# Spreading layer 0's projections, attention halves and low parts over its eight score tiles

## The chip, the core and the metric

One core of a Trainium2 chip runs the whole program. The metric is the device time of one execution in microseconds. All times of rows are microseconds from the start of the span unless they say ns. PE is TensorE, PEld its weight loads, DVE VectorE, ACT ScalarE, POOL GpSimd, and SP the engine that issues every DMA (SPq in the rows).

## What is computed

Two layers on x of shape (4, 256, 32, 32), that is 4 images of 256 channels by 1024 positions. All is float32.

```python
# layer 0, per image, xf = x.reshape(256, 1024)
Bm, Cm, Dm = Wb @ xf, Wc @ xf, Wd @ xf
S = softmax(Bm.T @ Cm, axis=-1)          # 1024 x 1024
y = gamma * (Dm @ S.T) + x
# layer 1: group norm, q/k/v projections, 4-head attention over 1024
# positions, output projection, residual; result = y + projection
```

## The kernel before

Every matmul of two float32 operands is split: a high part (the value copied into the type fp32r, made by ACT) and a low part (the value less its high part, made by DVE or POOL). A product is then the three matmuls high·high, low·high and high·low (`products`, L217).

**Layer 0, one image.** The scores are rows of S in eight tiles of 128 rows by 1024 columns (12 matmuls each, `scores0`, L1342), with A = x'(Wb'Wc) made once per image by the four groups a0 to a3 (6 matmuls each, `a_group`). Three tile buffers of PSUM hold them in turn (`score_tile`, L377). A tile then goes a long way round the engines:

1. DVE takes the row maximum (`row_max0`, L894).
2. ACT takes the exponential with its row sum (`exp0`, L677), and DVE the reciprocal (`recip0`, L899).
3. POOL multiplies the tile by it (`normalise0`, L580).
4. DVE transposes it in blocks of 32 by 32 (`turn`, L903, line L911 in rows) into `turned`, of two buffers.
5. SP stores it to DRAM (`store_turned`, L457, issue L460), and after the store has landed loads it back with the blocks in their turned places (`load_turned`, L462, four DMAs at L467) into `pt_lo`.
6. ACT copies it into `pt_hi` (`turn_high_of`, L683, line L685 in rows). The low part is the difference (`turn_difference`, L395, line L397 in rows): POOL makes it for tiles 0, 1, 2, 4, 5 and 6 of an image (`POOL_LOWS`), DVE for tiles 3 and 7 (`DVE_LOW`, L915).

Four tiles make one half of the result's columns. The groups av0 and av1 (24 matmuls each, `values`, L1350) use tiles 0 to 3, av2 and av3 tiles 4 to 7. Before av0, PE waits for the low parts of four tiles, before av2 for those of eight. DVE takes each group's result out of PSUM, adds the residual and takes statistics (`result`, L1057, lines L1063 and L1068), and SP stores it (`store_result`, L474).

All groups other than scores share two PSUM banks in turn (`place_groups`, L128), so that a group waits until the one before the last has been taken out (`bank_free`, L1245).

**The order** is written out by hand for each engine. PE runs a score tile and behind it one entry of `SCORES0` (L57): av2 and av3 of the image before, in halves, behind tiles 0 to 3, the projections d0 to d3 (12 matmuls each, D = Wd x, `project_d`) behind tiles 4 to 7. Then comes `TAIL0` (L62): av0 in quarters, av1, and the next image's a0 to a3, for which PE waits until the next image's x is split (`x_part_high`, L712, on ACT, and `x_part_low`, L1007, on DVE). The last image has `TAIL0_LAST` (L63) instead: av0, av1, then the first projections of layer 1 (qk0 to qk5) with av2 in thirds and av3 between them, then the first two score tiles of layer 1 (s0, s1). Each qk group is restacked by SP into `q_st` or `k_st` by four DMAs (`restack`, L438, issue L451), and the buffer of qk holds two groups, so that ACT waits before the third for the first's DMAs (`chunk_high`, L740).

ACT's order in layer 0 is `image0` at L755: exponentials, behind those of steps 2 to 5 the high parts of tiles 0 to 3, the d high parts behind steps 4 to 7, and after step 7 the high part of tile 4, x, tiles 5 and 6, then a0, tile 7, a1 to a3. POOL's is `image0` at L624: normalise tile t, and behind t = 3, 4, 5 the low parts of tiles 0, 1, 2, and 4, 5, 6 at the end. DVE's is `image0` at L1052: at step s the reciprocal of tile s-1, then up to step 4 the turning of tile s-1 before the maximum of tile s, from step 5 on the maximum before the turning. SP's is `image0` at L478: up to tile 3 each tile is stored and loaded, from tile 4 on the load of tile t-1 is issued behind the store of tile t. The first image has its own order, because nothing of an image before it exists.

Layer 1 (`image1`) runs 32 score tiles per image and is not touched.

## Time and profile before

| what | value |
|---|---|
| median of 3 runs | 727.3 us (724.44 to 727.85) |
| profiled execution, its own time | 727.05 us |
| its span | 725.3 us |
| PE busy | 681.8 us (94%) |
| PE weight loads busy | 567.3 us (78%) |
| DVE busy | 552.1 us (76%) |
| ACT busy | 454.9 us (63%) |
| POOL busy | 288.5 us (40%) |
| chain that ended last, by engine | PE 65%, DMA 11%, DVE 10%, issue 5%, ACT 4%, SPq 4% |

A busy share is an average over the whole span. Layer 0 takes about the first 278 us, layer 1 the rest. To see what bounds layer 0, its four images have to be looked at one by one. An engine's idle time is written in brackets behind the instruction that ended it, with what released it. The span is 1.75 us shorter than the execution's own time, and the difference lies around it.

### The profile page before, as it was taken

How to read it: one execution, taken by the hardware profiler on the slowest of the kernel's cores; microseconds unless marked ns; L12 is line 12 of the kernel's file. 1: busy time of each engine (PE TensorE's matmuls, PEld its weight loads, DVE VectorE, ACT ScalarE, POOL GpSimd, SP SyncE). 2: the span in 40 equal slices, each digit the busy share in tenths (PEclk: the TensorE clock that was granted, in tenths of full speed). 3: DMA queues.
4: the chain of work that ended last, by engine and by line, in shares of the span. 5: the costliest groups of instructions: out<-in, count | busy, mean ns of one | idle time of the engine just before them, and what ended most of it. 6: DMA issues, size and time to landing. Idle time of an engine off the chain costs nothing.

```text
span 725.3 us, 11325 instructions
## 1 busy us (share of the span) xinstructions
PE 681.8 (94%) x3632; PEld 567.3 (78%) x3632; DVE 552.1 (76%) x854; ACT 454.9 (63%) x788; POOL 288.5 (40%) x238
## 2 busy tenths in 40 slices
PE   4948999899999978999999999999999999999996
PEld 3746788688788766887888987887888888888885
DVE  3548556656765735999888889888889988889994
ACT  4344334325524324798777778877779877778883
POOL 0144234415516511356524356433346523334531
PEclk9989999899999999999999999999999999999999
DMA  8256557635845866700165401165501145501011
GB/s 272 89 156 197 171 189 224 194 127 192 240 166 175 243 158 150 203 1 1 44 160 132 131 16 45 44 139 129 154 14 43 29 119 129 130 15 44 7 47 36
DMA packets 52143, 86.32 MB, mean 119 GB/s; under 512 B 6016, under 2 KB 24704, under 8 KB 52096
## 3 DMA queue, kind: packets, MB, share of 16 engines
q1 hardware_dynamic: 52096, 85.75, 41.5%
q8 instruction: 22, 0.36, 0.2%
q14 instruction: 25, 0.20, 0.1%
HBM read 35.40 MB, written 25.17 MB: 83 GB/s over the span
## 4 chain that ended last, share of the span: by engine, by line
PE 65%; DMA 11%; DVE 10%; issue 5%; ACT 4%; SPq 4%; POOL 0%; ACTq 0%; DVEq 0%; POOLq 0%
PE acc L1241 33%; PE scores L1241 17%; PE trans L1275 14%; DMA turn_scratch<-turned 4%; DMA pt_lo<-turn_scratch 4%; SPq L467 3%; DVE negmax L887 2%; DVE turned L911 2%; DMA w_later<-in_wlater 1%; DVE negmax L896 1%; DVE pt_lo L930 1%; PE trans L1241 1%; ACT prob L694 1%; ACT pt_hi L704 1%; DMA k_st<-qk 1%
## 5 line engine op out<-in xcount | busy, mean ns | idle before, releaser
L593 POOL TENSOR_SCALAR prob<-prob,rsum 128x1024 f32<-128x1024 f32 x127 | 143.3, 1128 | 264.3 <-DVE rsum L892 264.3
L704 ACT ACTIVATE pt_hi<-trans 128x512 fp32r<-128x512 f32 x256 | 140.2, 595 | 62.9 <-PE trans L1275 60.2
L930 DVE TENSOR_TENSOR pt_lo<-trans,pt_hi 128x512 fp32r<-128x512 f32 x256 | 163.7, 680 | 3.1 <-ACT pt_hi L704 2.8
L887 DVE TENSOR_REDUCE negmax<-scores 128x1 f32<-128x1024 f32 x128 | 155.1, 1212 | 8.3 <-PE scores L1241 6.8
L694 ACT ACTIVATE prob<-scores,negmax 128x1024 f32<-128x1024 f32 x128 | 143.3, 1120 | 13.4 <-DVE negmax L887 11.8
L1275 PEld LDWEIGHTS trans<-ident,prob 128*128 128x128 f32 x1024 | 117.2, 140 | 28.7 <-DVE pt_lo L930 5.3
L1275 PE MATMUL trans<-ident,prob 128*128 128x128 f32 x1024 | 135.7, 274 | 4.1 <-DVE pt_lo L930 3.4
L1241 PE MATMUL scores<-k_st,q_st 128*128 128x512 f32 x512 | 137.8, 391 | 0.9 <-issue 0.5
L1241 PEld LDWEIGHTS scores<-k_st,q_st 128*128 128x128 f32 x512 | 95.8, 188 | 22.3 <-ACT prob L694 1.0
L1241 PE MATMUL acc<-pt_hi,v_st 128*128 128x512 f32 (+1 forms) x264 | 106.7, 407 | 1.9 <-DVE pt_lo L930 1.9
L1241 PE MATMUL acc<-pt_lo,v_st 128*128 128x512 f32 (+1 forms) x264 | 101.0, 385 | 0.0
L397 POOL TENSOR_TENSOR pt_lo<-pt_lo,pt_hi 128x1024 fp32r<-128x1024 f32 x24 | 59.9, 2498 | 18.2 <-ACT pt_hi L685 18.2
L1241 PE MATMUL acc<-pt_hi,d_hi 128*128 128x512 f32 x128 | 52.5, 410 | 7.6 <-DVE qk L1048 3.9
L685 ACT ACTIVATE pt_hi<-pt_lo 128x1024 fp32r<-128x1024 f32 x32 | 33.8, 1056 | 39.9 <-DMA pt_lo<-turn_scratch 39.7
L1241 PEld LDWEIGHTS acc<-pt_hi,v_st 128*128 128x128 f32 x264 | 49.8, 189 | 9.1 <-DVE pt_lo L930 2.1
L1241 PEld LDWEIGHTS acc<-pt_lo,v_st 128*128 128x128 f32 x264 | 50.0, 189 | 7.1
L583 POOL TENSOR_SCALAR prob<-prob,rsum 128x1024 f32<-128x1024 f32 x16 | 18.0, 1127 | 84.9 <-DVE rsum L901 84.9
L1241 PE MATMUL acc<-pt_lo,d_hi 128*128 128x512 f32 x128 | 51.6, 403 | 0.0
L1241 PE MATMUL acc<-pt_hi,d_lo 128*128 128x512 f32 x128 | 51.5, 403 | 0.0
L1241 PE MATMUL scores<-x_hi,a_hi 128*128 128x512 f32 x96 | 37.9, 395 | 1.0 <-ACT prob_more L680 1.0
L583 POOL TENSOR_SCALAR prob_more<-prob_more,rsum 128x1024 f32<-128x1024 f32 x16 | 18.0, 1126 | 52.1 <-DVE rsum L901 52.1
L680 ACT ACTIVATE prob<-scores,negmax 128x1024 f32<-128x1024 f32 x12 | 13.4, 1116 | 40.2 <-DVE negmax L896 40.2
(143 smaller groups left out, 1168.6 us busy)
## 6 DMA issues: line engine op xcount, KB each, us to landing
turn_scratch<-turned SPq DMA_DIRECT2D x32, 512.0 KB, 3.3
pt_lo<-turn_scratch SPq DMA_DIRECT2D x128, 128.0 KB, 3.4
k_st<-qk SPq DMA_DIRECT2D x64, 256.0 KB, 4.6
q_st<-qk SPq DMA_DIRECT2D x64, 128.0 KB, 2.4
x_raw<-in_x SPq DMA_DIRECT2D x8, 512.0 KB, 5.7
y_out<-in_x SPq DMA_DIRECT2D x16, 256.0 KB, 3.6
y_scratch<-y_out SPq DMA_DIRECT2D x16, 256.0 KB, 2.9
y_in<-y_scratch SPq DMA_DIRECT2D x4, 1024.0 KB, 7.5
```

What stands on the lines that cost most here:

```text
L397: return engine.tensor_tensor(turned_tile(pt_lo, t), turned_tile(pt_lo, t).bitcast(F32), turned_tile(pt_hi, t).bitcast(F32), ALU.subtract)
L467: sp.dma_start(dst.rearrange("c (q n) -> c q n", q=QUADS), blocks[g]).then_inc(turn_moved[t % 4], 16)
L583: nc.gpsimd.tensor_scalar(p, p, rsum[:, t % 4:t % 4 + 1], 1.0, ALU.mult, ALU.mult)\
L593: nc.gpsimd.tensor_scalar(p, p, rsum[:, t % 2:t % 2 + 1], 1.0, ALU.mult, ALU.mult)\
L685: nc.scalar.activation(turned_tile(pt_hi, t), turned_tile(pt_lo, t).bitcast(F32), ACT.Copy)\
L694: nc.scalar.activation(prob[:, t % 2, :], scores[:, t % 2, :], ACT.Exp, bias=negmax[:, t % 2:t % 2 + 1], scale=1.0, accum_out=rowsum[:, t ...
L704: nc.scalar.activation(pt_block(pt_hi, (t // 4) % 2, t, h), trans[:, h, :].rearrange("p (j n) -> p j n", n=P), ACT.Copy).then_inc(pt_high, 1)
L887: nc.vector.tensor_reduce(negmax[:, t % 2:t % 2 + 1], scores[:, t % 2, :], AX_X, ALU.max, negate=True).then_inc(max_ready, 1)
L911: nc.vector.transpose(turned[:, t % 2, :], prob_tile(t).rearrange("p (j g c) -> p g j c", g=QUADS, c=QUAD))\
L930: nc.vector.tensor_tensor(pt_block(pt_lo, slot, t, h), trans[:, h, :].rearrange("p (j n) -> p j n", n=P), pt_block(pt_hi, slot, t, h).bitc ...
L1241: ins = nc.tensor.matmul(dst, w, m, start=(starts and n == 0), stop=(stops and n == len(pairs) - 1))
L1275: ins = nc.tensor.transpose(trans[:, h, b * P:(b + 1) * P], prob[:, t % 2, j * P:(j + 1) * P], ident[:, :])
```

## The change

- PE: behind tile 4 come d0 and d1, behind tile 5 d2 and d3, behind tiles 6 and 7 the two halves of this image's own av0. The tail begins with av1. In the last image qk0 to qk3 follow av1 without a part of av2 between them, then av2, qk4, av3, qk5. The group a0 waits for the first half of the next x alone, a2 for the second.
- SP: in every image but the first, each tile is stored and then loaded before the next one is stored. In the first image load t-1 stands behind store t up to tile 3, from then on as in the others. The other DMAs take other places in the queue, and av0's result is stored right behind tile 7's load.
- Low parts: all eight on POOL, tile s-2 behind the normalising of tile s, except tile 3 (`URGENT`), which stands ahead of the normalising of tile 5. DVE makes none.
- ACT: the high part of tile s-2 behind the exponential (and the d parts) of step s, except tile 3, which stands ahead of the exponential of step 5. Tile 4 stands behind the exponential of step 6, tile 5 behind that of step 7, tile 6 behind the next x, tile 7 behind a1 (qk1).
- DVE: at step s the reciprocal of tile s-1, the d low parts (two at step 5, two at step 6), the turning of tile s-1, then the maximum of tile s. In the first image up to step 4 the maximum comes before the turning. av0's result is taken out right behind the next x (last image: behind the four parts of h).

```diff
-SCORES0 = [("prev_av2", 0, 2), ("prev_av2", 1, 2), ("prev_av3", 0, 2), ("prev_av3", 1, 2), "d0", "d1", "d2", "d3"]
-D_STEPS = [4, 5, 6, 7]
+BEHIND_SCORES0 = {0: [("prev_av2", 0, 2)], 1: [("prev_av2", 1, 2)], 2: [("prev_av3", 0, 2)], 3: [("prev_av3", 1, 2)],
+                  4: ["d0", "d1"], 5: ["d2", "d3"], 6: [("av0", 0, 2)], 7: [("av0", 1, 2)]}
+D_STEPS = {4: (0, 1), 5: (2, 3)}
-TAIL0 = FIRST_HALF + ["av1", "next_a0", "next_a1", "next_a2", "next_a3"]
-TAIL0_LAST = FIRST_HALF + ["av1", "next_qk0", "next_qk1", ("av2", 0, 3), "next_qk2", ("av2", 1, 3), "next_qk3",
-                           ("av2", 2, 3), "av3", "next_qk4", "next_qk5", "s0", "s1"]
+TAIL0 = ["av1", "next_a0", "next_a1", "next_a2", "next_a3"]
+TAIL0_LAST = ["av1", "next_qk0", "next_qk1", "next_qk2", "next_qk3", "av2", "next_qk4", "av3", "next_qk5", "s0", "s1"]
-POOL_LOWS, DVE_LOW = (0, 1, 2), 3
+URGENT = 3
...
@@ SP, image0
-                    if t == 4 and not first:
-                        store_result(i - 1, 3)
-                        sp.wait_ge(y_stored, FREE_CREDIT + i * 64)
-                        load_result_residual(i, 1)
                     store_turned(i, t)
-                    if t < 4 and not first:
-                        load_turned(i, t)
-                    elif t % 4 > 0:
+                    if first and t in (1, 2, 3):
                         load_turned(i, t - 1)
-                    if t == 7 or (first and t == 3):
+                    if not first or t >= 3:
                         load_turned(i, t)
                     if t == 1 and not first:
                         store_result(i - 1, 2)
+                    if t == 3 and not first:
+                        store_result(i - 1, 3)
+                    if t == 5 and not first:
+                        sp.wait_ge(y_stored, FREE_CREDIT + i * 64)
+                        load_result_residual(i, 1)
+                store_result(i, 0)
@@ POOL, image0
+                    behind = t - HIGH_BEHIND
+                    if behind == URGENT:
+                        turn_low_of(t0, behind)
                     normalise0(t0, t)
-                    if t - 3 in POOL_LOWS:
-                        turn_low_of(t0, t - 3)
+                    if behind >= 0 and behind != URGENT:
+                        turn_low_of(t0, behind)
...
-                for t in POOL_LOWS:
-                    turn_low_of(t0, t + 4)
+                for t in range(T0_IMAGE - HIGH_BEHIND, T0_IMAGE):
+                    turn_low_of(t0, t)
@@ ACT, image0
+                    behind = s - HIGH_BEHIND
+                    if behind == URGENT:
+                        turn_high_of(i, behind)
                     exp0(t0, s)
-                    if HIGH_BEHIND <= s < HIGH_BEHIND + 4:
-                        turn_high_of(i, s - HIGH_BEHIND)
+                    for n in D_STEPS.get(s, ()):
+                        high(d_part(d_hi, n), plan, f"d{n}")
+                    if behind >= 0 and behind != URGENT:
+                        turn_high_of(i, behind)
...
-                turn_high_of(i, 4)
                 if not last:
                     for half in range(X_HALVES):
                         x_part_high(i + 1, half)
-                turn_high_of(i, 5)
                 turn_high_of(i, 6)
-                if last:
-                    turn_high_of(i, 7)
...
-                    if name == "next_a0":
+                    if name in ("next_a1", "next_qk1"):
                         turn_high_of(i, 7)
@@ DVE, image0
-                    if 1 <= s <= 4:
+                    for n in D_STEPS.get(s - 1, ()):
+                        low(d_part(d_lo, n), d_part(d_hi, n), plan, f"d{n}", highs + plan.until(f"d{n}", KINDS0))
+                    dense = first and s <= 4
+                    if s >= 1 and not dense:
                         turn(i, s - 1)
...
                     row_max0(t0, s)
-                    if s == HIGH_BEHIND + 4:
-                        turn_low_of(t0, DVE_LOW)
-                    if s > 4:
+                    if s >= 1 and dense:
                         turn(i, s - 1)
...
+                result("av0", i)
@@ PE, image0
-                        pe.wait_ge(turn_low_pool, 6 * of + 3 * (half + 1))
-                        pe.wait_ge(turn_low, 2 * of + half + 1)
+                        pe.wait_ge(turn_low, T0_IMAGE * of + 4 * (half + 1))
                     if name == "av0":
-                        evacuated(plan.number(f"d{part}"))
+                        evacuated(plan.number(f"d{2 * part + 1}"))
...
-                        if n == 0:
-                            pe.wait_ge(x_split, X_HALVES * (i + 2))
+                        if n % 2 == 0:
+                            pe.wait_ge(x_split, X_HALVES * (i + 1) + n // 2 + 1)
```

## Rows read from the trace of the kernel before

**Rows 1.** Windows by image: stretch, length, busy us by engine, PEclk, DMA share, GB/s.

```profile
18.48:79.59 61.11, 47.91 (x218) 38.62 (x216) 36.35 (x45) 24.84 (x36) 23.52 (x14) 0.94 0.53 155
79.59:142.44 62.85, 59.21 (x265) 48.21 (x264) 39.19 (x45) 23.98 (x34) 24.11 (x14) 0.95 0.59 188
142.44:200.23 57.79, 57.07 (x265) 46.07 (x264) 37.02 (x45) 23.80 (x34) 24.25 (x14) 1.00 0.62 194
200.23:278.61 78.38, 72.54 (x329) 58.80 (x328) 42.36 (x69) 25.80 (x39) 27.68 (x19) 0.98 0.66 189
```

**Rows 2.** Timeline of PE, chosen matmuls: start us, us, what, [idle before <-releaser].

```profile
12.05 0.47 PE L1241 MATMUL acc<-x_hi,wbc_hi 128*128 128x512 f32 x1 [2.50 <-DVE wbc_lo L1029]
...
50.88 0.58 PE L1241 MATMUL acc<-wd_hi,x_hi 128*128 128x256 f32 x1 [8.13 <-DVE d_lo L1016]
...
85.15 0.39 PE L1241 MATMUL scores<-x_hi,a_hi 128*128 128x512 f32 x1
...
87.90 0.40 PE L1241 MATMUL acc<-pt_hi,d_hi 128*128 128x512 f32 x1
...
90.74 0.39 PE L1241 MATMUL trans<-x_hi,a_hi 128*128 128x512 f32 x1
...
104.66 0.28 PE L1241 MATMUL acc<-wd_hi,x_hi 128*128 128x256 f32 x1
...
106.09 0.40 PE L1241 MATMUL trans<-x_hi,a_hi 128*128 128x512 f32 x1
...
134.05 0.79 PE L1241 MATMUL acc<-x_hi,wbc_hi 128*128 128x512 f32 x1 [3.20 <-DVE y_out L1063]
...
259.57 0.76 PE L1241 MATMUL acc<-pt_hi,d_hi 128*128 128x512 f32 x1 [3.92 <-DVE qk L1048]
```

**Rows 3.** Timeline of ACT: high parts behind a load; a chunk of layer 1.

```profile
37.53 1.06 ACT L685 ACTIVATE pt_hi<-pt_lo 128x1024 fp32r<-128x1024 f32 x1 [3.27 <-DMA pt_lo<-turn_scratch]
...
112.85 1.06 ACT L685 ACTIVATE pt_hi<-pt_lo 128x1024 fp32r<-128x1024 f32 x1 [0.83 <-DMA pt_lo<-turn_scratch]
...
125.41 1.06 ACT L685 ACTIVATE pt_hi<-pt_lo 128x1024 fp32r<-128x1024 f32 x1 [3.37 <-DMA pt_lo<-turn_scratch]
...
264.61 0.69 ACT L746 ACTIVATE qk<-acc,vec 128x512 fp32r<-128x512 f32 x1 [5.95 <-PE acc L1241]
```

**Rows 4.** Timeline of SP: store and load of a tile, a later load, restacks.

```profile
104.93 0.34 SPq L460 DMA_DIRECT2D turn_scratch<-turned  x1
...
108.39 1.73 SPq L467 DMA_DIRECT2D pt_lo<-turn_scratch  x4
...
119.15 2.07 SPq L467 DMA_DIRECT2D pt_lo<-turn_scratch  x4
...
259.45 5.23 SPq L451 DMA_DIRECT2D q_st<-qk  x8
```

**Rows 5.** Timeline of DVE: turnings of images 0 and 1, x_lo, h_lo.

```profile
25.51 1.25 DVE L911 STREAM_TRANSPOSE turned<-prob 128x1024 f32<-128x1024 f32 x1 [1.45 <-POOL prob L583]
...
30.67 1.25 DVE L911 STREAM_TRANSPOSE turned<-prob 128x1024 f32<-128x1024 f32 x1 [1.36 <-POOL prob L583]
...
103.67 1.23 DVE L911 STREAM_TRANSPOSE turned<-prob_more 128x1024 f32<-128x1024 f32 x1
...
123.10 1.25 DVE L911 STREAM_TRANSPOSE turned<-prob_more 128x1024 f32<-128x1024 f32 x1 [0.34 <-POOL prob_more L583]
...
127.45 5.89 DVE L1010 TENSOR_TENSOR x_lo<-x_raw,x_hi 128x1024 fp32r<-128x1024 f32 x2 [3.10 <-ACT x_hi L715]
...
246.34 2.46 DVE L370 TENSOR_TENSOR h_lo<-y_in,h_hi 128x512 fp32r<-128x512 f32 x4
```

**Rows 6.** By line: x_lo low parts at the start; pt_lo on DVE, on POOL.

```profile
L1010 DVE TENSOR_TENSOR x_lo<-x_raw,x_hi x2: 1215/1220/1226, 10.1 to 11.9; 128x1024 fp32r<-128x1024 f32 x2
...
L397 DVE TENSOR_TENSOR pt_lo<-pt_lo,pt_hi x8: 1214/1217/1762, 56.4 to 257.5; 128x1024 fp32r<-128x1024 f32 x8
...
L397 POOL TENSOR_TENSOR pt_lo<-pt_lo,pt_hi x24: 2340/2406/3338, 41.2 to 255.1; 128x1024 fp32r<-128x1024 f32 x24
```

More of the change, by code:

```diff
@@ L327, in build @@
         turn_low = sem("turn_low")
-        turn_low_pool = sem("turn_low_pool")
         transposed = sem("transposed")
@@ L1383, in image0 @@
                         norm_group(plan, "gn1", 0, gn_sqdev, 1)
[L1384 to L1387 removed]
+                    for g in BEHIND_SCORES0[s]:
+                        if g in D_GROUPS:
+                            project_d(D_GROUPS.index(g))
+                        elif g[0] == "av0":
+                            values(g[0], i, *g[1:])
+                        elif not first:
+                            values(g[0], i - 1, *g[1:])
                 for g in TAIL0_LAST if last else TAIL0:
```

29 lines of the change are left out of this document (5 added, 24 removed).

## The prediction, made before the changed kernel was run

> **What bounds the kernel now.** The page says PE 94% busy, so I looked for PE's idle time. The windows by image [rows 1] show it in layer 0: from an image's first score tile to the next one's it takes 61.11, 62.85 and 57.79 us, and 78.38 us for the last image up to layer 1's first scores. The third has PE busy for 57.07 us at full clock, so 57 us is near what an image costs when nothing waits.
>
> The PE timeline [rows 2] gives the pieces. A score tile takes 2.75 us (85.15 to 87.90), half an av group 2.84, a d group 1.43 (104.66 to 106.09), so an a group of half as many matmuls as a score tile takes 1.4. Per image: 8 x 2.75 + 4 x 5.68 + 4 x 1.43 + 4 x 1.4 = 56.0. What is above it are stalls: 8.13 us before d2 in image 0, 3.20 before a0 in image 1, 3.92 in the last image, where the DVE, queued behind tile 7's low part, is late with qk. [...]
>
> The ACT and SP rows tell why. Tile 3's high part starts at 112.85, that is 33.3 us into its image [rows 3]: store at 104.93, landed and load issued at 108.39, load in at 112.85, 4.5 us later [rows 4]. Tile 4's load, sharing the DMA engines with another store, needs 6.3 us (119.15 to 125.41) [rows 3, 4]. x's high and low parts stand behind it. That is the stall before a0.
>
> **The change, part by part.** I write times from the image's first score tile.
>
> *PE's order.* No matmul is added. Tiles 4 to 7 now come every 5.6 us (2.75 + 2 x 1.43, or 2.75 + 2.84) instead of 4.2. S5 ends at 30.7, S6 at 36.3.
>
> *Tile 3 ahead.* Tiles 0 to 3 keep their pace, order and queue, so tile 3's load is in at 33.1 as before. ACT could start exponential 5 at 32.1 (S5's end and a maximum of 1.2), but takes tile 3 first: 33.1 to 34.1, the exponential to 35.4. POOL takes low 3 first too, 2.40 us [rows 6]: 34.2 to 36.6. Normalising 5 follows to 37.7, turning 5 from 37.9 to 39.1. On DVE it would have ended at 36.3, so tile 5 is 2.8 us late. PE can start av0 at 36.8, a stall of only 0.5.
>
> *The round.* From tile 5 on the maximum stands behind the turning of the tile before, so a tile costs a whole round: maximum, exponential, reciprocal, normalising, turning. The rounds of image 0, in that order already, take 5.16 us (25.51 to 30.67) [rows 5]. PE gives 5.6, so only 0.4 is regained per tile. Turning 7 ends at 39.1 + 2 x 5.2 = 49.5. Before, it ended at 44.8 (124.35 less 79.59) [rows 5].
>
> *x and av0's result.* The x parts come behind turning 7. Low 5 sits on POOL from 48.4 (behind normalising 7) to 50.8. An x_lo takes 1.22 alone; the two of image 1 took 5.89 beside POOL's lows [rows 5, 6], so they wait for each other. I take: the first ends 1.1 behind low 5, at 51.9, the second at 53.1 (bounds 52.0 with no such wait, 55.4 with the 5.89). Then av0's result, 0.75: 53.9, and a0 may start at 54.0. PE, with av0 from 36.8, S7 and av1, is done at 50.9. **A stall of 3.1 us before a0**, nearest to the row of 3.20, so I price it like that one: next image at 54.0 + 8.4 = 62.4. Images 1 and 2 come to 124.8, before 120.6: +4.2.
>
> *Image 0.* With the maximum ahead of the turning, exponentials 1 and 2 come 2.5 and 5 us earlier, and then ACT stands in front of tile 0's high part. Its load goes out at about 30 instead of 32.3, so ACT has it at 35 to 36 instead of 37.53 [rows 3]. Exponential 4 is at 38.5, d0's low part at 41.3, and d2 starts at about 42.4 instead of 50.88: the stall of 8.13 becomes one of about 4. Tile 3's load goes out at 44, in at 49; low 3 ends near 52.5, a second stall of about 4 before av0. Then rounds of 5.2: turning 7 ends at 65.3, a0 starts near 70.5, image 1 near 76.5 instead of 79.6: -3.1. This counts 1.4 to 1.7 of slow matmuls behind each of the two.
>
> *Last image.* The four low parts of h (2.46 alone, 246.34) [rows 5] now stand between turning 7 (48.9, gn0 and gn1 included) and av0's result. No row shows them beside a POOL low that started first: bounds 0 and 2.4, I take 1.5 as for x_lo. qk0 starts at 54.3. [...] qk0 to qk3 run together, 5.6 us, and then av2 needs qk2's bank. qk2's high part waits for qk0's DMAs: 5.2 us from issue to ACT (259.45 to 264.61) [rows 3, 4]. av2 starts about 11 us behind qk0, a stall of 3.6 where 3.92 was, with the same clock loss. From there 2 x 5.68 + 2 x 1.4 = 14.2. Sum 80.5 against 78.4 (200.2 to 278.6): +2.1.
>
> *At nothing:* DVE rid of two lows (1.22 each [rows 6]) wins nothing, since it waits for tiles. The a2 gate, the moved result stores and residual loads (an issue of 0.4 to 0.9 each) lie beside the round on a queue that needs 3.5 + 1.75 per tile of 5.6; without that slack each would delay a tile by itself. Layer 1 starts from the same state.
>
> Sum: -3.1 + 4.2 + 2.1 = +3.2 on 727.05, the profiled execution, which lies 0.25 under the median of the three runs. **Forecast 730.2.**
>
> **The rivals.**
>
> *The clock holds.* The stall of 3.1 lies between the idle times that kept the clock (2.50) and lost it (3.20) [rows 2]. If it keeps it, images 1 and 2 take 60.1 (54.0 + 5.6 + 0.5) and the last image loses 0.7 less: 730.2 - 4.6 - 0.7 = 725. [...]
>
> *No stall at all.* Tile 3's data come early enough that ACT loses nothing, and the rounds of tiles 6 and 7 fit. Then images 1 and 2 take 56.6 (-7.4), image 0 58 (-3.1), the last image about 76 (-2.4): 714. Against it: tile 3's way is in the old trace at 33.3, and nothing of the change shortens it. Half of that would give 721.
>
> *Loads as slow as tile 4's.* Tile 3's load takes 6.3 instead of 4.5 because results, residuals and the next x share the engines with it. It decides from any microsecond on: ACT, POOL and PE all stand behind this one load, so its 1.8 us come four times, in image 0 also for tile 0: 730.2 + 4 x 1.8 + 1.3 = 739. For it: 6.3 in the row. Against it: tile 3 itself, at 4.5, had the same neighbours.
>
> **How the numbers follow.** Forecast 40%, clock holds 25%, no or half a stall 17%, slow loads 18%. About 0.5%, 3.6 us, is what a measurement of this kernel can tell from no change: faster is below 723.7, slower above 730.9. The forecast's own range is 727 to 733 (bounds of x_lo and h_lo), a third of it slower, so slower is 0.18 + 0.14 = 0.32. Faster is 0.17 and a little of the clock case: 0.20. Same 0.48. The range goes from 719 to 738: it leaves out the full case without stalls and the end of the slow one.
>
> **What would show it.** Right: in images 1 and 2 ACT waits for a DMA before tile 3's high part and exponential 5 behind it; the turnings of tiles 5, 6 and 7 are 5.2 apart and the last ends 49 to 50 into the image; PE is idle for about 3 us before a0, released by DVE's y_out; image 0 has two stalls of about 4 us instead of one of 8; in the last image av2's first matmul waits for DVE qk. Wrong: no idle time before a0, or tile 3's high part starting clearly before 33; then I have its load or the order behind it wrong, and the time goes toward 714.

## The result, and the profile after

| what | before | after |
|---|---|---|
| median of 5 runs | 726.87 us (724.44 to 727.85) | 731.24 us (729.96 to 732.35) |
| ratio, 95% interval | | 1.0064 [1.0041, 1.0087] |
| profiled execution, its span | 727.05, 725.3 us | 732.35, 730.6 us |

The changed kernel is 0.64% slower, just over the 0.5% that the prediction took as what can be told. Two more runs of before put its median at 726.87 instead of 727.3. The forecast was 730.2 with a range of 719 to 738. Five executions taken for the experiments were disturbed (one 1.8% above the fastest of its kernel, the others 17% to 138%), and the medians below leave them out.

The page of the changed kernel, its busy line, its chain and ACT's high parts of loaded tiles:

```profile
PE 684.2 (94%) x3632; PEld 568.4 (78%) x3632; DVE 541.3 (74%) x846; ACT 453.3 (62%) x788; POOL 304.2 (42%) x246
...
PE 63%; DVE 9%; DMA 8%; issue 7%; POOL 5%; ACT 5%; SPq 2%; ACTq 0%; DVEq 0%; POOLq 0%
...
L686 ACT ACTIVATE pt_hi<-pt_lo 128x1024 fp32r<-128x1024 f32 x32 | 33.8, 1055 | 56.2 <-DMA pt_lo<-turn_scratch 56.2
```

POOL is busier by 15.7 us and DVE less by 10.8; the eight low parts that moved are worth 19.2 and 9.7 us by [rows 6]. In the chain, POOL with 5% is new (0% before), and the DMA share fell from 11% to 8%. ACT spends 56.2 us standing before tiles' loads. Where the time lies is seen again in the windows by image, the columns being those of [rows 1]:

```profile
20.15:77.10 56.95, 48.13 (x217) 39.32 (x216) 32.71 (x41) 23.52 (x35) 25.48 (x15) 0.94 0.52 157
77.10:139.42 62.32, 58.62 (x266) 47.21 (x265) 35.06 (x42) 23.15 (x34) 28.05 (x16) 0.97 0.57 182
139.42:200.75 61.33, 57.15 (x266) 45.96 (x264) 34.56 (x42) 23.38 (x34) 27.98 (x16) 1.00 0.58 189
200.75:283.93 83.18, 73.92 (x329) 59.28 (x328) 41.23 (x67) 26.97 (x40) 34.34 (x22) 0.96 0.64 190
```

Against [rows 1] the images changed by -4.16, -0.53, +3.54 and +4.80 us. The first score tile starts at 20.15 instead of 18.48, +1.67. What follows image 3 takes 446.67 instead of 446.69. That makes the +5.3 of the span. The third window is the plainest: PE is busy for 57.15 us at a granted clock of 1.00, as before (57.07), but the image takes 61.33 us.

The timeline of PE of the changed kernel, the matmuls before which it stood idle:

```profile
43.95 0.58 PE L1230 MATMUL acc<-wd_hi,x_hi 128*128 128x256 f32 x1 [4.41 <-DVE d_lo L1011]
54.34 0.79 PE L1230 MATMUL acc<-pt_hi,d_hi 128*128 128x512 f32 x1 [3.18 <-POOL pt_lo L395]
...
114.56 0.50 PE L1230 MATMUL acc<-pt_hi,d_hi 128*128 128x512 f32 x1 [0.28 <-POOL pt_lo L395]
131.79 0.51 PE L1230 MATMUL acc<-x_hi,wbc_hi 128*128 128x512 f32 x1 [2.85 <-DVE y_out L1058]
143.51 0.50 PE L1230 MATMUL acc<-pt_hi,d_hi 128*128 128x512 f32 x1 [1.21 <-POOL pt_lo L395]
...
194.50 0.50 PE L1230 MATMUL acc<-x_hi,wbc_hi 128*128 128x512 f32 x1 [2.36 <-DVE y_out L1058]
...
240.04 0.50 PE L1230 MATMUL acc<-pt_hi,d_hi 128*128 128x512 f32 x1 [1.30 <-POOL pt_lo L395]
256.90 0.47 PE L1230 MATMUL acc<-h_hi,wq_hi 128*128 128x512 f32 x1 [2.50 <-DVE y_out L1058]
267.65 0.77 PE L1230 MATMUL acc<-pt_hi,d_hi 128*128 128x512 f32 x1 [4.47 <-DVE qk L1043]
```

The 8.13 us before d2 in image 0 [rows 2], with another 1.72 before av0 (at 60.09 in the kernel before), became 4.41 and 3.18. Images 1 and 2 both have a stall before a0 now, and one of 1.21 stands before the av2 that runs in image 2, where there was none. The last image has three; before, it had 3.92 before av2 and 1.43 before av0 (at 241.31).

The rows behind the stall before a0 in image 1, of ACT, POOL and DVE:

```profile
110.89 1.06 ACT L686 ACTIVATE pt_hi<-pt_lo 128x1024 fp32r<-128x1024 f32 x1 [3.39 <-DMA pt_lo<-turn_scratch]
111.86 1.10 ACT L681 ACTIVATE prob<-trans,negmax 128x1024 f32<-128x1024 f32 x1
```

```profile
112.03 2.40 POOL L395 TENSOR_TENSOR pt_lo<-pt_lo,pt_hi 128x1024 fp32r<-128x1024 f32 x1 [2.04 <-ACT pt_hi L686]
114.42 1.11 POOL L581 TENSOR_SCALAR prob<-prob,rsum 128x1024 f32<-128x1024 f32 x1
...
126.44 2.41 POOL L395 TENSOR_TENSOR pt_lo<-pt_lo,pt_hi 128x1024 fp32r<-128x1024 f32 x1 [0.43 <-ACT pt_hi L686]
```

```profile
115.57 1.25 DVE L910 STREAM_TRANSPOSE turned<-prob 128x1024 f32<-128x1024 f32 x1 [0.71 <-POOL prob L581]
...
120.89 1.25 DVE L910 STREAM_TRANSPOSE turned<-prob_more 128x1024 f32<-128x1024 f32 x1 [1.53 <-POOL prob_more L581]
...
126.05 1.25 DVE L910 STREAM_TRANSPOSE turned<-prob_more 128x1024 f32<-128x1024 f32 x1 [1.37 <-POOL prob_more L581]
127.35 3.72 DVE L1005 TENSOR_TENSOR x_lo<-x_raw,x_hi 128x1024 fp32r<-128x1024 f32 x2
```

ACT stands before tile 3's load with exponential 5 behind it, POOL makes low 3 before it normalises 5, and so the turning of 5 starts 38.5 us into the image (115.57 less 77.10). The rounds that follow are 5.32 and 5.16 apart. This is the chain that the prediction drew. Beside it SP shows what it did not draw, the tail of the tiles on its queue:

```profile
122.88 0.90 SPq L469 DMA_DIRECT2D y_out<-in_x  x2
123.89 0.36 SPq L458 DMA_DIRECT2D turn_scratch<-turned  x1
129.69 1.75 SPq L465 DMA_DIRECT2D pt_lo<-turn_scratch  x4
131.56 0.36 SPq L458 DMA_DIRECT2D turn_scratch<-turned  x1
```

Tile 6 was turned at 122.14. Its store went out at 123.89, behind the residual load, and had landed only at 129.69, 5.8 us later; tile 7, turned at 127.30, was stored at 131.56. Over layer 0 the waits of SP for a store to land went from the first of these lines, of before, to the second, of after (us in all, times, longest):

```profile
SPq L467 <- DMA turn_scratch<-turned: 43.6, 21, 3.5
```

```profile
SPq L465 <- DMA turn_scratch<-turned: 90.4, 29, 5.3
```

### The profile page after: what moved, and what is told of

It reads as the page before. It is cut to its first block, busy times and chain, and to the rows that moved or that the text cites. A ratio compares the mean times of both kernels' runs of the same rounds, so it can differ in the third digit from the quotient of the medians.

```text
span 730.6 us, 11320 instructions
## 1 busy us (share of the span) xinstructions
PE 684.2 (94%) x3632; PEld 568.4 (78%) x3632; DVE 541.3 (74%) x846; ACT 453.3 (62%) x788; POOL 304.2 (42%) x246
## 4 chain that ended last, share of the span: by engine, by line
PE 63%; DVE 9%; DMA 8%; issue 7%; POOL 5%; ACT 5%; SPq 2%; ACTq 0%; DVEq 0%; POOLq 0%
PE acc L1230 32%; PE scores L1230 15%; PE trans L1264 14%; DMA turn_scratch<-turned 5%; POOL pt_lo L395 3%; DMA pt_lo<-turn_scratch 2%; DVE turned L910 2%; DVE negmax L886 2%; SPq L465 2%; DVE pt_lo L925 1%; PE trans L1230 1%; DVE negmax L895 1%; ACT prob L695 1%; DMA x_raw<-in_x 1%; POOL prob_more L581 1%
## 5 line engine op out<-in xcount | busy, mean ns | idle before, releaser
L695 ACT ACTIVATE prob<-scores,negmax 128x1024 f32<-128x1024 f32 x128 | 143.3, 1119 | 13.4 <-DVE negmax L886 11.8
L395 POOL TENSOR_TENSOR pt_lo<-pt_lo,pt_hi 128x1024 fp32r<-128x1024 f32 x32 | 76.5, 2389 | 52.2 <-ACT pt_hi L686 52.1
L686 ACT ACTIVATE pt_hi<-pt_lo 128x1024 fp32r<-128x1024 f32 x32 | 33.8, 1055 | 56.2 <-DMA pt_lo<-turn_scratch 56.2
L1230 PE MATMUL acc<-pt_hi,d_hi 128*128 128x512 f32 x128 | 53.6, 419 | 11.3 <-POOL pt_lo L395 6.8
L1230 PEld LDWEIGHTS acc<-pt_lo,v_st 128*128 128x128 f32 x264 | 49.9, 189 | 7.1
L900 DVE RECIPROCAL rsum<-rowsum 128x1 f32<-128x1 f32 x32 | 5.2, 162 | 50.7 <-ACT prob L681 28.4
L1230 PEld LDWEIGHTS acc<-pt_hi,d_hi 128*128 128x128 f32 x128 | 24.9, 195 | 20.1 <-POOL pt_lo L395 5.3
L581 POOL TENSOR_SCALAR prob<-prob,rsum 128x1024 f32<-128x1024 f32 x16 | 18.0, 1123 | 53.6 <-DVE rsum L900 53.6
L1230 PE MATMUL scores<-x_hi,a_lo 128*128 128x512 f32 x96 | 37.5, 391 | 0.0
```

Of the source, the lines that this page charges most:

```text
L395: return engine.tensor_tensor(turned_tile(pt_lo, t), turned_tile(pt_lo, t).bitcast(F32), turned_tile(pt_hi, t).bitcast(F32), ALU.subtract)
L581: nc.gpsimd.tensor_scalar(p, p, rsum[:, t % 4:t % 4 + 1], 1.0, ALU.mult, ALU.mult)\
L686: nc.scalar.activation(turned_tile(pt_hi, t), turned_tile(pt_lo, t).bitcast(F32), ACT.Copy)\
L695: nc.scalar.activation(prob[:, t % 2, :], scores[:, t % 2, :], ACT.Exp, bias=negmax[:, t % 2:t % 2 + 1], scale=1.0, accum_out=rowsum[:, t ...
L1230: ins = nc.tensor.matmul(dst, w, m, start=(starts and n == 0), stop=(stops and n == len(pairs) - 1))
```

## The experiments

Two limits had to be told apart. **The round**: DVE comes late to x and to av0's result because turning 7 is late (maximum behind the turning, tile 3 ahead of 5, POOL's low parts). **The queue**: with one tile at a time, tiles 6 and 7 are late, and what ACT and PE have behind them waits. **The cover** is a third reading: PE has 8.5 us of work between tile 7's scores and a0 (half of av0, and av1) where it had 11.4. The experiments ran in three groups, each on one chip with the kernel before beside it: e1, e2, e4 and e5, then e6, e3, e7 and e8, then e10, e9, e11 and e12. The kernel before had medians of 726.07, 725.12 and 725.8 in them. Image lengths are from each profile, from one image's first score tile to the next one's.

| kernel | images 0 to 3, us | median | ratio to before |
|---|---|---|---|
| after | 56.95, 62.32, 61.33, 83.18 | 731.24 | 1.0064 [1.0041, 1.0087] |
| e1 av0's result early | 57.37, 63.44, 59.68, 83.62 | 731.61 | 1.0078 [1.0049, 1.0107] |
| e2 tile 3 not ahead | 62.78, 59.16, 59.88, 80.35 | 732.21 | 1.0091 [1.0067, 1.0115] |
| e4 residual load late | 57.16, 62.27, 59.32, 82.21 | 731.31 | 1.0060 [1.0031, 1.0088] |
| e3 old last tail | 57.33, 62.87, 61.47, 83.50 | 732.72 | 1.0115 [1.0056, 1.0175] |
| e7 maximum first | 57.62, 62.81, 60.95, 83.43 | 732.98 | 1.0109 [1.0059, 1.0160] |
| e8 DVE's lows back | 57.10, 62.04, 60.30, 81.60 | 729.75 | 1.0070 [1.0040, 1.0099] |
| e10 av0 behind tile 7 | 58.66, 61.50, 61.46, 80.06 | 731.93 | 1.0105 [1.0064, 1.0147] |
| e9 three places | 55.41, 64.47, 60.70, 83.21 | 731.93 | 1.0090 [1.0056, 1.0124] |
| before + e5 | 59.23, 58.88, 57.79, 78.06 | 723.20 | 0.9960 [0.9929, 0.9991] |
| before + e11 | 65.67, 67.49, 65.95, 86.24 | 752.30 | 1.0372 [1.0337, 1.0408] |
| before + e12 | 56.42, 58.30, 57.30, 74.80 | 714.93 | 0.9854 [0.9828, 0.9880] |

**e1: take av0's result before tile 7's last steps on DVE**

```diff
@@ DVE, image0, behind the maximum of tile s
+                    if s == T0_IMAGE - 1:
+                        result("av0", i)
...
-                result("av0", i)
```

> The changed kernel with one edit: the DVE takes av0's result behind the maximum of tile 7, while it would wait for the exponential, instead of behind both x_lo parts. My theory (the DVE's order at the image's end makes the stall before a0): the first x_lo part ends about 1.1 us before the second, and 0.75 of the result goes too, so the stalls of 2.85 and 2.35 us before a0 in images 1 and 2 fall to about 1.1 and 0.8, image 1 no longer loses the clock (another 1.9), and the last image's stall before qk0 falls by 0.75: in all 5 us less than the changed kernel, about 726 us. Rival (the slow loads of tiles 6 and 7 are the real limit and hold the next image's av2): the stall before a0 goes, but comes back in front of av2, and the time stays within 1.5 us of 731.

The stall before a0 fell from 2.85 and 2.36 us to 1.06 and 0.94, released by x_lo. A new one of 2.85 and 1.44 came later in the a groups. In image 1, PE and ACT:

```profile
137.49 0.80 PE L1231 MATMUL acc<-x_hi,wbc_hi 128*128 128x512 f32 x1 [2.85 <-DVE a_lo L1011]
```

```profile
135.16 1.06 ACT L686 ACTIVATE pt_hi<-pt_lo 128x1024 fp32r<-128x1024 f32 x1 [5.72 <-DMA pt_lo<-turn_scratch]
```

ACT stood before tile 6's load for 5.72 us, with a's high parts behind it, and until a0's high and low parts are made a2 has no PSUM bank. So a0 started 53.0 us into the image instead of 54.7, but a2 at 59.3 instead of 59.4: the queue lies close behind the first limit, and the edit is worth nothing in the median.

**e2: tile 3 has no place ahead**

```diff
-URGENT = 3
+URGENT = None
```

> The changed kernel with tile 3's high and low parts behind step 5's exponential and normalising, like the other tiles. My theory (ACT standing in front of tile 3's load before exponential 5 delays the rounds of tiles 5 to 7 by about 2.5 us): turning 7 ends 2 to 3 us earlier in its image, the stall before a0 shrinks to about 1.2 us, but av0 waits 1.3 us more for low 3, so the time changes by less than 2 us against 731. Rival (the urgent place pays for itself, because av0 stands on low 3): av0's stalls grow by more than the stall before a0 shrinks, 734 us or more.

Images 1 and 2 are 3.16 and 1.45 us shorter: the stall before a0 is 0.81 and 0.80, at the price of 1.42 before av0. This shows that tile 3's place carries most of that stall. The last image is 2.8 us shorter too. Image 0 pays most of it back, 5.8 us more (4.37 before av0, then 3.07 before a0), and the median does not tell this kernel from the changed one.

**e4: the residual load behind the image's last tile**

```diff
@@ SP, image0
-                    if t == 5 and not first:
-                        sp.wait_ge(y_stored, FREE_CREDIT + i * 64)
-                        load_result_residual(i, 1)
+                if not first:
+                    sp.wait_ge(y_stored, FREE_CREDIT + i * 64)
+                    load_result_residual(i, 1)
```

> The changed kernel with the second residual load (512 KB) issued behind tile 7's load instead of in front of tile 6's store. My theory: tile 6's store, 5.8 us from issue to landing in image 1, falls to about 3.5 and tile 7's load lands 2 us earlier, which takes away the stalls of 0.4, 1.2 us before av2 and part of the 4.5 us before av2 of the last image (1 us, because there qk2's bank comes free only 0.3 us before low 7): about 728.5 us. Rival (the slow landing has another cause, the loads of tile 5 or the order of DRAM reads and writes): no change, 731.

SP's rows of image 1, in place of those shown of after:

```profile
123.44 0.36 SPq L458 DMA_DIRECT2D turn_scratch<-turned  x1
127.02 1.73 SPq L465 DMA_DIRECT2D pt_lo<-turn_scratch  x4
```

The store of tile 6 lands in 3.58 us, not 5.8. ACT has tile 6 at 131.43 instead of 134.21, and the stall before av2 in image 2 is gone (-2.0 us for that image, 1.2 of them this stall). The stall before a0 is there as before, 2.47 and 2.37. So the residual load is what made tile 6 late, and it has no part in a0's stall. In the median nothing is left of it that the intervals could show.

**e5: in the kernel before, image 0's maximum ahead of the turning**

```diff
@@ DVE, image0
-                    if 1 <= s <= 4:
+                    dense = first and s <= 4
+                    if 1 <= s <= 4 and not dense:
                         turn(i, s - 1)
...
-                    if s > 4:
+                    if s > 4 or (s >= 1 and dense):
                         turn(i, s - 1)
```

> The kernel before with one part of the change alone: in image 0, up to tile 4, the maximum ahead of the turning. My theory (half of image 0's gain of 4 us comes from this order, until ACT stands in front of tile 0's load): exponential 3 comes 1.5 us earlier, tile 4's 3 to 5 us, the stall of 8.13 us before d2 falls to 4 to 5 us and the image ends about 3 us earlier: 724 us. Rival (the gain of image 0 comes from the places of d0 to d3 and of the SP queue): less than 1 us, 726.5.

Image 0 is 1.9 us shorter, but not by the way that was expected: the stall before d2 is 7.92 us where it was 8.13. The gain lies before two score tiles (0.62 and 0.98 became one of 0.36) and before av0 (1.72 became 0.61). The median is 2.9 us under that of before, and the interval ends just below 1. The 58.88 of image 1 against 62.85 can hardly be the edit's, which touches image 0 alone: its stall before a0 was 0.50 in this execution, 3.20 in that of before. The two profiled executions lie 6.2 us apart where the medians lie 2.9 apart, so a part of that difference is chance, and the 62.85 is a doubtful base for image 1. Of the 4.16 us that image 0 gained in the changed kernel this order gives about half; e12 shows where the rest is.

**e6: e1 and e4 together**

```diff
@@ SP, image0: as e4
@@ DVE, image0: as e1
```

> The two edits of e1 and e4 together on the changed kernel: av0's result behind the maximum of tile 7, and the second residual load behind tile 7's load. Alone, neither moved the time. My theory now (two queues end the image almost at once: the DVE with av0's result, and ACT, which stands in front of tile 6's load before it can take a0 out; each hides the other): images 1 and 2 need both, and take about 59 us each instead of 62.3 and 61.3, the last image about 82, in all 725 to 727 us. Rival (each edit has a cost of its own that ate its gain, such as av0's result in front of tile 7's reciprocal): 731 or more again.

Median 728.4 us, ratio 1.0045 [1.0013, 1.0078], the lowest of the variants of the changed kernel but not told apart from its 1.0064, and above the 725 to 727 us that two limits hiding each other should have given. Its profiled execution took 738.0 us, so its images are not read, and it has no row in the table.

**e3: the old tail in the last image**

```diff
-TAIL0_LAST = ["av1", "next_qk0", "next_qk1", "next_qk2", "next_qk3", "av2", "next_qk4", "av3", "next_qk5", "s0", "s1"]
+TAIL0_LAST = ["av1", "next_qk0", "next_qk1", ("av2", 0, 3), "next_qk2", ("av2", 1, 3), "next_qk3",
+              ("av2", 2, 3), "av3", "next_qk4", "next_qk5", "s0", "s1"]
```

> The changed kernel with the last image's tail in the old order, av2 in thirds between the qk groups. My theory (av2 stands on tile 7's low part, ready at 266.5 in the changed kernel, 0.3 us before qk2's bank): av2 starts about 1 us earlier, but qk2 and qk3, 2.8 us of PE, now lie behind the stall and not in it, so the last image takes 1 to 3 us more, 732 to 734 us. Rival (the bank and the restacks are the limit of the new order): the stall before av2 falls from 4.5 to 3 us or less and the kernel is 2 us faster, 729.

The last image takes 83.50, +0.3. A part of av2 now waits 5.84 us for POOL's low 7 where the whole of it waited 4.47 for qk. av2 starts 2.4 us earlier, 64.5 us into the image, but qk2 and qk3, 2.8 us of PE's work, now lie behind the stall and not ahead of it. The order of the tail is not what costs.

**e7: maximum ahead of the turning for tiles 5 to 7 too**

```diff
-                    dense = first and s <= 4
+                    dense = (first and s <= 4) or s > 4
```

> The changed kernel with the maximum ahead of the turning from step 5 on, as in the kernel before. The forecast's theory (the round of 5.2 us per tile makes the end of the image late): turning 7 ends about 3 us earlier and the stall before a0 goes, 726 us. Rival, which a walk over the durations gives: tile 5's load lands when it did, ACT stands in front of it before the next x's high parts, and the x_lo parts and the stall before a0 stay as they are, 730 to 732 us, with turning 7 about 3 us earlier all the same.

Turning 7 starts 48.4 us into image 1 (48.95 in the changed kernel), and the stall before a0 is 2.42 and 1.95. Only 0.5 us came back, because tile 7's scores stand behind half of av0 on PE: DVE waited 3.02 us for them before maximum 7. The order of maximum and turning makes the rounds 5.2 us long, but PE's own spacing of 5.6 is next to it, and so the order alone costs 0.5. Nor did a0 gain by it (55.3 us into image 1, 54.7 in the changed kernel), for x then waited for ACT, which had stood 1.97 us before tile 5's load with x's high parts behind it:

```profile
128.21 3.71 DVE L1005 TENSOR_TENSOR x_lo<-x_raw,x_hi 128x1024 fp32r<-128x1024 f32 x2 [1.21 <-ACT x_hi L716]
```

This is the rival that stood beside the expectation.

**e8: low parts 3 and 7 back on DVE**

```diff
@@ POOL, image0
-                for t in range(T0_IMAGE - HIGH_BEHIND, T0_IMAGE):
+                for t in (6,):
...
@@ DVE, image0
                     row_max0(t0, s)
+                    if s == 5:
+                        turn_low_of(t0, 3)
...
+                    if name in ("next_a1", "next_qk1"):
+                        turn_low_of(t0, 7)
```

> The changed kernel with the low parts of tiles 3 and 7 on the DVE again (1.2 us instead of 2.4): tile 3's behind the maximum of tile 5, tile 7's behind a1 (qk1). The forecast's theory (low 3 on POOL holds normalising 5 by about 1 us and so every later round): turning 7 ends 1 us earlier in images 1 and 2, the stall before av0 goes (0.3 to 1.3 us) and the one before a0 falls by 1 us; tile 7's low part is ready 1.2 us earlier: 727 to 729 us. Rival (POOL has room, where the low parts are made does not matter): 731.

The stall before av0 in image 0 is 2.02 (3.18), that before av2 in the last image 3.61 (4.47). The stall before a0 stays, 3.34 and 1.83. The images together take 261.04 us against 263.78, but the ratio overlaps that of the changed kernel: what POOL's 2.4 us for a low part against DVE's 1.2 costs is at most near 3 us, and not resolved.

**e10: both halves of av0 behind tile 7**

```diff
-                  4: ["d0", "d1"], 5: ["d2", "d3"], 6: [("av0", 0, 2)], 7: [("av0", 1, 2)]}
+                  4: ["d0", "d1"], 5: ["d2", "d3"], 6: [], 7: [("av0", 0, 2), ("av0", 1, 2)]}
```

> The changed kernel with both halves of av0 behind tile 7, so that score tile 7 follows tile 6 at once. New theory (cover): what counts is how much PE work lies behind score tile 7, because its maximum, exponential, normalising and turning, the next x and av0's result come after it one by one; the spreading cut that cover from 11.4 us (av0 and av1) to 8.5. Alone this edit gives the cover back, but the round of 5.2 us per tile, with the maximum behind the turning, keeps turning 7 where it is (49 to 50 us into the image): images 1 and 2 stay at 61 to 62.5 us, the time at 730 to 732. Rival (the maximum order never mattered, PE's place of tile 7 alone set turning 7): turning 7 moves 2 us or more ahead and the kernel gets to 727 or less.

The cover is 11.4 us again. The stalls before av0 are gone (0.70 us is left in image 0), and those before a0 are 5.09, 3.45 and 2.88. a0 of image 1 starts 54.0 us into it, 54.7 in the changed kernel. More cover only moves PE's idle time, since a0 waits for DVE, and turning 7 still starts at 48.75 into the image. By itself, cover is not the reason; e9 needs it together with e7's order and an earlier x.

**e9: e10, e7, and tile 5's high part behind x on ACT**

```diff
@@ PE: as e10; DVE: as e7; ACT, image0
-                    if behind >= 0 and behind != URGENT:
+                    if behind >= 0 and behind != URGENT and behind != 5:
...
+                turn_high_of(i, 5)
                 turn_high_of(i, 6)
```

> The changed kernel with three places put back: both halves of av0 behind tile 7, the maximum ahead of the turning from step 5 on, and the next x's high parts ahead of tile 5's. Cover theory: turning 7 starts 44 to 45.5 us into images 1 and 2 instead of 49, x is split by 48, and there is no stall before a0. The loads of tiles 6 and 7, one by one on the queue at 5.3 us or more a tile, then come to the front: a stall of 1 to 3 us before the next image's av2. Images 1 and 2 take 58 to 60 us, the time is 725 to 728. Rival (something else holds a0: the low parts on POOL, or tile 6's load through ACT): a stall of 2 us or more stays before a0, 730 or more.

Here the round gives way, as DVE of image 1 (from 74.85) shows:

```profile
121.27 1.25 DVE L911 STREAM_TRANSPOSE turned<-prob_more 128x1024 f32<-128x1024 f32 x1 [2.33 <-POOL prob_more L581]
122.44 2.31 DVE L1006 TENSOR_TENSOR x_lo<-x_raw,x_hi 128x1024 fp32r<-128x1024 f32 x2
```

Turning 7 starts at 46.4, the x parts are done at 49.9, and there is no stall before a0. But ACT and PE:

```profile
132.44 1.06 ACT L686 ACTIVATE pt_hi<-pt_lo 128x1024 fp32r<-128x1024 f32 x1 [7.58 <-DMA pt_lo<-turn_scratch]
```

```profile
134.76 0.79 PE L1231 MATMUL acc<-x_hi,wbc_hi 128*128 128x512 f32 x1 [5.31 <-DVE a_lo L1012]
```

All that was won stands in one wait, 7.58 us of ACT for tile 6. The store of tile 6 was issued at 121.92, right behind the residual load, and had landed at 127.97. The stall has only moved from a0 to a2, and its release from the round to the queue.

**e11: in the kernel before, the change's queue order alone**

```diff
@@ SP, image0
-                    if t < 4 and not first:
-                        load_turned(i, t)
-                    elif t % 4 > 0:
+                    if first and t in (1, 2, 3):
                         load_turned(i, t - 1)
-                    if t == 7 or (first and t == 3):
+                    if not first or t >= 3:
                         load_turned(i, t)
```

> The kernel before with the change's order of stores and loads alone (each tile stored and then loaded, the other DMAs where they were). Theory: with score tiles every 4.2 us a queue that needs 5.3 us a tile falls behind; tile 4's load comes about 1 us earlier and shortens the stall before a0, tile 7's comes 2 to 4 us later and holds a0 to a3 through ACT and the next av2: 0 to 5 us slower, 729 us. Rival (this order is what gives the change its gain in image 0): 2 us or more faster, 723 or less.

It costs 26.5 us (752.3 less 725.8), where 0 to 5 had been expected. PE of the old order gives a tile every 4.2 us, and the loads of tiles 4 to 7 go out at 123.87, 130.35, 135.81 and 141.21, that is 5.4 to 6.5 apart. The waits of SP, the same line as the two above, and the worst stall of PE:

```profile
SPq L467 <- DMA turn_scratch<-turned: 89.9, 29, 5.1
```

```profile
284.05 0.76 PE L1239 MATMUL acc<-pt_hi,d_hi 128*128 128x512 f32 x1 [10.23 <-DVE qk L1046]
```

The same 90 us of waits are in the changed kernel, where tiles come every 5.6 us and layer 0 is 21.6 us shorter than here. So one tile at a time costs 26.5 us in PE's old order, and spreading the tiles, with what goes with it, nearly pays for it. What it costs in the spread order was not measured.

**e12: the kernel before, with image 0's order, the d parts first and the last image's tile 7 behind qk1**

```diff
@@ DVE, image0: as e5
@@ ACT, image0
                     exp0(t0, s)
+                    if s in D_STEPS:
+                        n = D_STEPS.index(s)
+                        high(d_part(d_hi, n), plan, f"d{n}")
                     if HIGH_BEHIND <= s < HIGH_BEHIND + 4:
                         turn_high_of(i, s - HIGH_BEHIND)
...
-                    if s in D_STEPS:
-                        n = D_STEPS.index(s)
-                        high(d_part(d_hi, n), plan, f"d{n}")
...
-                if last:
-                    turn_high_of(i, 7)
...
-                    if name == "next_a0":
+                    if name in ("next_a0", "next_qk1"):
                         turn_high_of(i, 7)
@@ DVE, image0: low 7 behind qk1 instead of ahead of qk0
```

> The kernel before with the parts of the change that the runs speak for: the maximum ahead of the turning in image 0 up to tile 4, and ACT's d high parts ahead of the high part of a tile; in the last image the high and low part of tile 7 behind qk1's instead of ahead of qk0's. Theory: in image 0 d0 and d1 are taken out before ACT stands in front of tile 2's load, the stall of 7.9 us before d2 falls to 3 or 4, and the first restacks of layer 1 go out 3 us earlier: 3 to 5 us less than the run with the maximum's place alone (723), 718 to 720 us. Rival (the stall only moves on to av0, which stands on tile 3's low part): 722 to 723 us.

It beats both kernels, and its own forecast of 718 to 720: 714.93 us (712.88 to 716.13), 10.9 under before. Its windows, columns as in [rows 1], and the largest stall left outside image 0:

```profile
17.57:73.99 56.42, 47.28 (x218) 38.22 (x216) 37.57 (x45) 24.84 (x36) 23.27 (x14) 0.97 0.58 166
73.99:132.29 58.30, 56.88 (x265) 46.01 (x264) 38.11 (x45) 23.81 (x34) 23.88 (x14) 1.00 0.62 198
132.29:189.59 57.30, 56.67 (x266) 46.03 (x264) 38.15 (x45) 23.84 (x34) 24.37 (x14) 1.00 0.66 202
189.59:264.39 74.80, 71.12 (x329) 57.71 (x328) 43.91 (x69) 25.82 (x39) 28.83 (x19) 1.00 0.69 199
```

```profile
246.74 0.47 PE L1238 MATMUL acc<-pt_hi,d_hi 128*128 128x512 f32 x1 [3.09 <-DVE pt_lo L397]
```

Three parts of it are the change's own: image 0's order, the d parts ahead of a tile's high part, tile 7 behind qk1. Without the new queue order they gain 1.5%. Image 0 differs from that of e5 by the d parts alone, and takes 56.42 instead of 59.23. PE is idle there for 9.1 us instead of 10.5, with 1.72 before d2, 2.84 before d3 and 3.92 before av0 in place of 7.92 before d2; the other half is PE's busy time, 47.28 instead of 48.75 us, at a granted clock of 0.97 instead of 0.91. Image 1, at 58.30, had 0.51 us before a0, much as in e5, so its 4.6 us against the kernel before are not put down to these edits. In the last image, where tile 7's place counts too, it is 74.80 against 78.06; how these 3.3 us divide was not tried.

## Why the prediction was right, and where it was not

Times are again from an image's first score tile.

**The sum: close, and in part by luck.** In the profiled execution image 0 came out 1.1 us under its term and images 1 and 2 together 1.2 under, the last image was 2.7 over, and 1.7 at the start stood in no term. These nearly cancel; the medians differ by +4.4 where +3.2 was forecast.

**Tile 3 and the round: right.** Tile 3 reached ACT at 33.8 (forecast 33.1), PE started av0 at 37.5 (36.8), the rounds took 5.32 and 5.16 (5.2), turning 7 ended at 50.2 (49.5), and a0 started at 54.7 (54.0). The 0.7 of tile 3 went through unchanged. e2 shows the cause: with tile 3 not ahead the stall before a0 is 0.8. In image 2 tile 3 came at 34.7 and a0 at 55.1. x's low parts took 3.72 us beside POOL's low 5 (forecast 3.6 from turning 7's end to theirs), and 2.31 in e9, where none ran beside them. The 5.89 of the kernel before, which the forecast kept as a bound, had a second low part of POOL that began inside the pair:

```profile
129.46 2.80 POOL L397 TENSOR_TENSOR pt_lo<-pt_lo,pt_hi 128x1024 fp32r<-128x1024 f32 x1 [0.50 <-ACT pt_hi L685]
```

**The stall before a0: right in size, its clock in one image of two.** Forecast 3.1 us; measured 2.85 and 2.36. Priced like the row of 3.20, the next image should have come 8.4 us behind a0: in the kernel before it did (134.05 to 142.44, the a matmuls 0.43 us apart and the granted clock 0.50 until 139.7), where the forecast counts 5.6 for four a groups that wait for nothing. It came 7.63 behind in image 1 (granted clock 0.78 over them) and 6.25 in image 2 (1.00). That is the rival in which the clock holds, in one image. The two took 123.65 against 124.8. Image 1's 62.32 against 62.4 hides two misses, a0 0.7 us later and the way behind it 0.8 shorter.

The chance of that rival was set with a row that was misread. The 2.50 us at 12.05 [rows 2] do not show a pace that was kept, for it was low before them. The matmuls ahead of that wait, such as the last one, come 0.21 us apart for 256 columns, where a d group of the same size takes 1.43 for twelve, 0.12 apart (the granted clock reads 1.00 in both stretches):

```profile
9.14 0.41 PE L1241 MATMUL acc<-wc_lo,wb_hi 128*128 128x256 f32 x1
```

Behind it they come 0.23 us apart for 512 columns. So their pace per column about doubled by the end of that wait, and no row of the kernel before bounds from below what a stall may last.

**Image 0: right in its times, short in its cause.** d2 started 23.8 us behind the first score tile (forecast 23.9), av0 34.2 (34.0), turning 7 ended at 46.8 (46.8), a0 started at 50.9 (52.0). The image took 56.95 against 58.0; the 1.1 lies between turning 7's end and a0, where x_lo and av0's result took 4.1 us and the sum had 5.2. But the prediction names only the maximum ahead of the turning. e5 has that alone and keeps 7.92 us before d2; the d parts ahead of a tile's high part on ACT, which the change also has, are what takes them away (e12).

**The last image: the sum of terms failed by 2.7 us.** Forecast 80.5, measured 83.18. The step that failed is "turning 7 (48.9, gn0 and gn1 included)": it ended at 51.9. The forecast's own 49.5 for images 1 and 2 had no gn0 in it, so the 48.9 was too early from the start, and in the kernel before the parts of h began 46.1 us into the last image, where turning 7 ended 44.8 into image 1. Against the 50.2 of image 1 the last image is 1.7 later, and tile 3 brought that: its high part came at 35.7 instead of 33.8. PE's idle time for gn0 is 0.72 of the 1.9; the store took 4.14 us to land instead of 3.34, which is 0.8, and the load 0.4 more. The rounds behind it stayed at 5.15 us each, so av0's wait for low 3 (1.30) has no part in it. Rows of tile 3 on SP and ACT:

```profile
231.66 1.73 SPq L465 DMA_DIRECT2D pt_lo<-turn_scratch  x4
```

```profile
236.47 1.06 ACT L686 ACTIVATE pt_hi<-pt_lo 128x1024 fp32r<-128x1024 f32 x1 [3.99 <-DMA pt_lo<-turn_scratch]
```

Rows of DVE, POOL and SP at the image's end:

```profile
251.42 1.25 DVE L910 STREAM_TRANSPOSE turned<-prob_more 128x1024 f32<-128x1024 f32 x1 [1.36 <-POOL prob_more L581]
252.59 3.50 DVE L368 TENSOR_TENSOR h_lo<-y_in,h_hi 128x512 fp32r<-128x512 f32 x4
```

```profile
251.35 2.40 POOL L395 TENSOR_TENSOR pt_lo<-pt_lo,pt_hi 128x1024 fp32r<-128x1024 f32 x1
```

```profile
258.31 1.73 SPq L465 DMA_DIRECT2D pt_lo<-turn_scratch  x4
261.03 5.57 SPq L449 DMA_DIRECT2D q_st<-qk  x8
```

The four parts of h took 3.50 instead of 2.46, 1.04 more where I took 1.5, and qk0 started at 56.15 instead of 54.3. (The forecast's terms, 48.9 + 2.46 + 1.5 + 0.75, make 53.6; the other 0.7 has no source in it, and 49.5 in place of 48.9 would give 54.2.) No row of the kernel before showed them beside a POOL low that had started first, and 1.5 was an estimate; here low 5 had started 1.24 us ahead and ran beside them for their first 1.16 us, until 253.75. They ended at 256.09, 2.34 us later, where alone they take 2.46, so they gained little while it ran. av2 then came 10.75 us behind qk0 (forecast 11), after a stall of 4.47, and its 24 matmuls took 7.99 us (granted clock 0.50 from 267.65 to 272) in place of the 5.84 that av3's took from 276.87 on. Behind it the forecast had 15.2 us including the lost clock, and it was 16.3. So: +1.85, -0.25, +1.1. The restack of qk0, whose last part DVE had done by 260.08, went out at 261.03 behind tile 7's load and a result's store, and ACT waited 2.00 us for it before qk2: the queue again. From issue to ACT it was 5.0 us (261.03 to 266.03), near the 5.2 of the forecast, but that figure had been read off a row in which ACT waited for PE (264.61, released by acc) and not for the restack. Low 7 ended at 266.45, 1.2 us before av2 could start, so tile 7 itself leaves little more than a microsecond to be won there.

**The start: +1.67 that no step had.** It lies in code that the change leaves alone. In the kernel before, the matmuls of the first a groups came 0.23 us apart from 12.05 on; in the changed kernel they stood 0.43 us apart until about 16.4 (granted clock 0.50 from 13 to 16). All nine variants of the changed kernel and e5 began them at 0.43 us as well (until 14.4 to 17.5), e11 and e12 did not. The first score tile came at 18.64 to 20.84 in the ten traces of the changed kernel and its variants, and at 17.57 to 18.72 in the four of the kernel before and its own. Whether the change has a hand in this or it is chance, no run here shows. The median is +4.4 where this execution is +5.3.

**"At nothing": wrong, and in the sum hardly seen.** I had the queue's 3.5 + 1.75 us per tile fit into tiles of 5.6, and put moved loads at nothing. A store behind the residual load takes 5.8 us to land, and tiles 6 and 7 come late: 1.21 us before av2 in image 2. e4 shows that it is this load. More important is what it hides. e1 and e9 shorten the round, and the queue at once puts its own stall of up to 5.31 us in the place; e11 gives the order's full price, 26.5 us without the spreading. The rival of slow loads, which would have put the 6.3 us on tile 3, did not come: the load took 4.4 us in image 1 and 4.8 in the last. That e1, e4, e7 and e10 each move no median fits two limits this close to each other. What shows the limits is the stalls in the traces of e1 and e9; no median does, since e6, which moves both, is not told apart from the changed kernel.

**Left open.** e9 with the residual load late, which by these rows should free both limits, was not tried, and e6's median leaves open what lifting both is worth. The spread order of PE with the old queue order, which would separate the two parts fully, was not tried either. It is also open how e12's gain in the last image divides, and what makes the start slow.

## What to carry to other kernels

When work is spread evenly so that an engine never waits, count the whole round of the longest chain against the new spacing, and do the same for the DMA queue, each tile from store to landed store to issued load: here 5.2 and 5.4 us against 5.6 left no room, and one more 512 KB load in front of a store used it up. A stall that two limits hold within a microsecond of each other answers to no single edit (e1 brought a0 1.7 us forward and a2 0.15), so look at what the next wait would be before giving one up. An engine that stands before a transfer with its other work behind it (ACT 3.39 us before tile 3, in e9 7.58 before tile 6) should first get everything that is ready and that somebody waits for; moving the d parts that way is a part of the version that won.

## What the runs showed of the hardware that was not expected

**A store landed later with a residual load ahead of it.** Issued 0.1 us behind a tile's load, 512 KB land in 3.6 us (e4, 123.44 to 127.02). With a residual load of 512 KB between that load and the store they need 5.8 us (after, 123.89), 6.05 (e9, 121.92) and 5.1 (after, last image, 247.78 to 252.84).

**The same idle time loses the clock or keeps it.** Before the a groups of image 2, 2.36 us kept the full pace in the changed kernel (194.50, shown above; the matmuls behind it 0.23 us apart, granted clock 1.00 in the window). In e3, 2.38 us did not (0.43 apart, granted clock 0.50 from 194 to 196), and in e7 even 1.95 did not, where the clock was still up for a microsecond and the granted clock was 0.50 from 194.6 on. In e9 it held through 3.41 us (1.00 from 72.00 to 74.85). The rows are from e3, e7 and e9:

```profile
193.19 0.80 PE L1231 MATMUL acc<-x_hi,wbc_hi 128*128 128x512 f32 x1 [2.38 <-DVE y_out L1059]
```

```profile
193.59 0.50 PE L1230 MATMUL acc<-x_hi,wbc_hi 128*128 128x512 f32 x1 [1.95 <-DVE y_out L1058]
```

```profile
72.00 0.47 PE L1231 MATMUL acc<-x_hi,wbc_hi 128*128 128x512 f32 x1 [3.41 <-DVE a_lo L1012]
```

The waits of 1.95 and 2.38 us lost it and the one of 3.41 did not, so the length of an idle time alone doesn't decide. A clock loss should be priced as a chance, here 1.4 us before a0 (7.63 against 6.25) and 2.1 before av2 (7.99 against 5.84).

**The clock column can miss the slow start.** In e10 the granted clock reads 1.00 in every microsecond from 11 to 15, while the a matmuls there stand 0.43 us apart, against 0.23 later on. At the start of an execution the spacing of the matmuls says more.
